# Three units per scan and per product, a smaller fine grid and a transposed residual in a convolution and Mamba kernel

## The reference

```
# layer 0: upsample 64x64 to a fine grid by FFT, pointwise network, low-pass, back to 64x64
h = upsample(x)
h = h @ W1.T + b1                              # 96 -> 384
h = coef[:, 0] + coef[:, 1] * h + coef[:, 2] * (h * h)
h = h @ W2.T + b2                              # 384 -> 96
out = lowpass(h)[::2, ::2]
# layer 1: Mamba over the 4096 positions of a sample
xs, z = split(u @ W_in.T);  xc = silu(causal_conv3(xs) + conv_b)      # 192 channels
dt, B, C = split(xc @ W_x.T);  delta = softplus(dt @ W_dt.T + b_dt)
h_t = exp(delta_t * A) * h_(t-1) + delta_t * B_t * xc_t               # 192 x 16 states
y_t = sum over the 16 states of h_t * C_t
out = ((y + xc * D) * silu(z)) @ W_out.T
```

## Time and profile before

| | |
|---|---|
| time, median of 3 runs (lowest to highest) | 6339.48 us (6336.2 to 6344.21) |
| the profiled execution, first to last instruction | 6343.7 us |
| busy: PE, DVE, POOL, ACT | 6036.5, 5685.5, 5209.8, 5097.3 us |
| DMA moved | 983.25 MB, 155 GB/s |

### The profile page before, as it was taken

How to read it: one execution, slowest core, us unless ns; L and a number is a source line. 1 busy time by engine, 2 the same in 40 slices (tenths; PEclk the granted TensorE clock), 3 DMA queues, 4 the chain that set the end, 5 groups by cost and what they waited for, 6 DMA issues and landing times. The chain is left out here.

```text
span 6343.7 us, 99100 instructions
## 1 busy us (share of the span) xinstructions
PE 6036.5 (95%) x32260; PEld 3123.0 (49%) x32260; DVE 5685.5 (90%) x4459; ACT 5097.3 (80%) x8658; POOL 5209.8 (82%) x5092
## 2 busy tenths in 40 slices
PE   8999999999999999999999999999999999998776
PEld 5645445454554545545455544545455454554222
DVE  0089999999999999999999999999999999999998
ACT  4588888888888888888888788888888888887664
POOL 0078888888888888888888888888888888888988
PEclk9999999999999999999999999999999999998665
DMA  3367676676767667675676767667676766767553
GB/s 95 88 165 170 160 167 157 163 162 169 169 154 168 155 165 170 155 182 142 167 162 162 173 156 169 155 164 163 167 169 156 166 154 165 168 142 160 129 124 75
DMA packets 805826, 983.25 MB, mean 155 GB/s; under 512 B 391258, under 2 KB 417542, under 8 KB 805318
## 3 DMA queue, kind: packets, MB, share of 16 engines
q1 hardware_dynamic: 805318, 976.92, 65.4%
HBM read 717.71 MB, written 259.00 MB: 154 GB/s over the span
## 5 line engine op out<-in xcount | busy, mean ns | idle before, releaser
L1181 POOL TENSOR_TENSOR hc<-hs,cs 128x512 f32<-128x512 f32 x3072 | 3835.6, 1271 | 692.7 <-DVE hs L1140 505.6
L1140 DVE TENSOR_TENSOR_SCAN hs<-av,state,b 128x512 f32<-128x512 f32 x2688 | 3257.8, 1263 | 88.6 <-POOL state L1185 4.9
L1008 ACT ACTIVATE av<-rep_d,nega 128x512 f32<-128x512 f32 x3072 | 2096.7, 713 | 41.5 <-DVE hs L1140 36.8
L1134 DVE TENSOR_TENSOR b<-rep_u,pb 128x1536 f32<-128x1536 f32 x1024 | 1803.5, 1761 | 211.0 <-PE pb L846 124.7
L855 PE MATMUL py<-hc,rsel 128*32 128x512 f32 x6144 | 1141.6, 634 | 40.6 <-POOL hc L1181 39.7
L769 PE MATMUL cb<-xu,w1a 96*128 96x392 f32 x2400 | 984.3, 513 | 27.7 <-DVE b1a L1120 17.4
L774 PEld LDWEIGHTS cb<-w2c,g 128*98 128x98 f32 x9600 | 885.9, 167 | 169.7 <-issue 106.9
L774 PE MATMUL cb<-w2c,g 128*98 128x96 f32 x9600 | 910.7, 252 | 17.4 <-ACT g L956 9.3
L956 ACT ACTIVATE g<-cb,b1a 128x392 f32<-128x392 f32 x1200 | 679.5, 579 | 87.0 <-PE cb L769 78.8
L810 PE MATMUL cb<-xn,wtap 96*96 96x512 f32 x1536 | 723.3, 607 | 2.4 <-ACT xn L1029 2.4
L769 PEld LDWEIGHTS cb<-xu,w1a 96*128 96x128 f32 x2400 | 414.5, 191 | 415.4 <-issue 199.3
(11 more groups left out here) (109 smaller groups left out, 6703.4 us busy)
## 6 DMA issues: line engine op xcount, KB each, us to landing
rep_d<-delta_scratch SPq DMA_DIRECT2D x512, 384.0 KB, 7.0
rep_u<-deltax_scratch SPq DMA_DIRECT2D x512, 384.0 KB, 6.3
cs<-c_scratch SPq DMA_DIRECT2D x512, 256.0 KB, 5.9
delta_scratch<-dlt SPq DMA_DIRECT2D x128, 384.0 KB, 3.1
deltax_scratch<-dlt SPq DMA_DIRECT2D x128, 384.0 KB, 9.2
t1r<-t_scratch SPq DMA_DIRECT2D x160, 240.0 KB, 6.5
v_scratch<-v2s SPq DMA_DIRECT2D x192, 192.0 KB
xb<-in_x SPq DMA_DIRECT2D x128, 192.0 KB, 4.6
```

Of the source, the lines that this page charges most:

```text
L1008: act.activation(av[:, n % NAV, :], rep_d[:, k % 2, j, :], ACT.Exp, scale=nega[:, q, j:j + 1])\
L1134: dve.tensor_tensor(b3[:, :, :], rep_u[:, k % 2, 3 * hf:3 * hf + 3, :], pb[:, None, :].broadcast_to([128, 3, T]), ALU.mult).then_inc(dve_b ...
L1140: dve.tensor_tensor_scan(hs[:, n % NHS, :], av[:, n % NAV, :], b3[:, n % 3, :], start, ALU.mult, ALU.add)\
L1181: pool.tensor_tensor(hc[:, n % NHC, :], hs[:, n % NHS, :], cs[:, k % 2, g % NQ, :], ALU.mult)\
```

## The change

- **Scan and product.** DVE makes one scan of 128x1536 per group, POOL one product of 128x1536. The scan runs through three units, so the state must not leak from one to the next: column 0 of every `av` is set to zero once (ACT fills columns 1 to 511), and column 0 of `b` is written as rep_u * pb + carry by a small scalar_tensor_tensor (128x3) ahead of the product for the other columns. `carry = exp(nega * rep_d[0]) * state` is prepared once per chunk: `first_x` on POOL (at unit 5, it needs the next chunk's rep_d), `first_a` on ACT (unit 15), two products on POOL (units 14 and 23). In a sample's first chunk there is no carry and no small operation. `av` has 9 buffers, so three groups.
- **Grid.** 98 x 97 points: 24 groups of four columns and one of two.
- **Residual.** x1o is transposed into the bank by PE ahead of the two products, in place of a product with the identity behind them; the planner's OUT goes from 2.70 to 2.25.

```
-GW, GH = 100, 98
-NB = GW // 4
+GW, GH = 98, 97
+NB = (GW + 3) // 4
-NHC, NAV, NHS = 6, 8, 6
+NHC, NAV, NHS = 6, 9, 6
...
-    "act": dict(xn=10, y=(18, 6), d=11, mid=23, batch=16),
+    "act": dict(xn=10, y=(18, 6), d=11, mid=23, batch=16, first=15),
-    "pool": dict(u=23, bc=(18, 22), y=(17, 8)),
+    "pool": dict(u=23, bc=(18, 22), y=(17, 8), first=5, carry=(14, 23)),
...  PE, OUT
+                    pe.transpose(o, x1o[:, tb], ident[0:C, 0:C])
                     for t in range(2):
-                        pe.matmul(o, xcs[:, p, t, tb], wo[:, t, :], start=(t == 0), stop=False)
-                    mm = pe.matmul(o, x1o[:, tb], ident[0:C, 0:C], start=False, stop=True)
+                        mm = pe.matmul(o, xcs[:, p, t, tb], wo[:, t, :], start=False, stop=(t == 1), skip_group_check=True)
...
-                act.wait_ge(dve_h, count(dve_h, G * NU + n + 1 - NAV))
-                act.activation(av[:, n % NAV, :], rep_d[:, k % 2, j, :], ACT.Exp, scale=nega[:, q, j:j + 1])\
+                act.wait_ge(dve_h, count(dve_h, G * NG + n // 3 + 1 - NAV // 3))
+                i = (G * NU + n) % NAV
+                act.activation(av[:, i, 1:T], rep_d[:, k % 2, j, 1:T], ACT.Exp, scale=nega[:, q, j:j + 1])\
...
+                lo = 0
+                if k > 0:
+                    lo = 1
+                    dve.wait_ge(pool_carry, count(pool_carry, (s * (NC8 - 1) + k - 1) * 2 + hf + 1))
+                    dve.scalar_tensor_tensor(b3[:, :, 0], rep_u[:, k % 2, js, 0], pb[:, 0:1], carry[:, q, js],
+                                             ALU.mult, ALU.add).then_inc(dve_c, 1)
+                dve.tensor_tensor(b3[:, :, lo:T], rep_u[:, k % 2, js, lo:T],
+                                  pb[:, None, lo:T].broadcast_to([128, 3, T - lo]), ALU.mult).then_inc(dve_bu, 1)
+                dve.wait_ge(pool_st, count(pool_st, G * NG + g + 1 - NHS // 3))
+                dve.wait_ge(act_a, count(act_a, G * NU + n + 3))
...
+                dve.tensor_tensor_scan(hs[:, h:h + 3, :].rearrange("p j t -> p (j t)"),
+                                       av[:, a:a + 3, :].rearrange("p j t -> p (j t)"),
+                                       b3[:, :, :].rearrange("p j t -> p (j t)"), 0.0, ALU.mult, ALU.add)\
...
-                pool.wait_ge(dve_h, count(dve_h, G * NU + n + 1))
-                pool.tensor_tensor(hc[:, n % NHC, :], hs[:, n % NHS, :], cs[:, k % 2, g % NQ, :], ALU.mult)\
+                pool.wait_ge(dve_h, count(dve_h, G * NG + g + 1))
+                pool.tensor_tensor(hc[:, p:p + 3, :], hs[:, h:h + 3, :],
+                                   cs[:, k % 2, q, None, :].broadcast_to([128, 3, T]), ALU.mult).then_inc(pool_hc, 1)
```

More of the change, by code:

```diff
@@ L30, with wide @@
 RING = 3
+def wide(b):
+    return min(4, GW - 4 * b)
 BATCH = 8
@@ L78 @@
 PE_US = {"ST": 0.45, "SA": 0.70, "SB": 0.70, "W_up": 0.70, "W_f": 0.71, "W_2": 2.10, "W_dn": 0.75, "D_lo": 1.20, "D_hi": 1.20,
-         "X": 2.72, "Z": 0.92, "DBC": 1.82, "DT": 0.50, "OUT": 2.70, "WARM": 0.215}
+         "X": 2.72, "Z": 0.92, "DBC": 1.82, "DT": 0.50, "OUT": 2.25, "WARM": 0.215}
 PE_PB, PE_RED = 0.22, 1.00
@@ L295, in build @@
         fcst = hs[:, 4, 0:NF]
-        state = sb("state", [128, NG, 3])
-        zero_state = sb("zero_state", [128, 1])
+        state = sb("state", [128, NQ, NJ])
+        first_x = sb("first_x", [128, NQ, NJ])
+        first_a = sb("first_a", [128, NQ, NJ])
+        carry = sb("carry", [128, NQ, NJ])
         os_ = sb("os_", [128, 4, C])
@@ L500, in _ @@
             load_xb(0, 0)
-            sp.dma_start(up_w[:, :, :], A["up_w"]).then_inc(ld_s, 16)
+            for r in range(2):
+                sp.dma_start(up_w[64 * r:64 * r + 64, :], A["up_w"][64 * r:64 * r + 64, r]).then_inc(ld_s, 16)
             load_xb(0, 1)
@@ L757, in step @@
                 elif name == "W_up":
-                    for e in range(2):
+                    for e in range(wide(b) // 2):
                         i2 = 2 * b + e
@@ L779, in step @@
                         half = slice(HH * (e % 2), HH * (e % 2) + HH)
-                        mm = pe.matmul(bank[half, 0:4 * C], dn_h[:, :], vr[:, e % 2, :], start=True, stop=True)
+                        n = wide(e) * C
+                        mm = pe.matmul(bank[half, 0:n], dn_h[:, :], vr[:, e % 2, 0:n], start=True, stop=True)
                 elif name == "DG":
@@ L824, in batched @@
                 rows = slice(32 + 64 * t, 32 + 64 * t + RANK)
-                return pe.matmul(bank[0:C, :], wdt[rows, C * t:C * t + C], dbc[rows, :], start=True, stop=True)
+                return pe.matmul(bank[0:C, :], wdt[rows, :], dbc[rows, :], start=True, stop=True)
             def out(st, k, bank):
@@ L1038, in c_part @@
             def c_part(st, k, n):
+                if n == AT["act"]["first"] and 0 <= st.s and k + 1 < NC8:
+                    c = st.s * (NC8 - 1) + k
+                    act.wait_ge(pool_first, count(pool_first, c + 1))
+                    act.wait_ge(pool_carry, count(pool_carry, c * 2))
+                    act.activation(first_a[:, :, :], first_x[:, :, :], ACT.Exp).then_inc(act_first, 1)
                 if n == AT["act"]["d"] and 0 <= st.s * NC8 + k + 1 < NS * NC8:
@@ L1138, in unit @@
[L1138 to L1140 removed]
+                    if G == 0:
+                        dve.wait_ge(av_set, count(av_set, 1))
+                dve.wait_ge(pe_b, count(pe_b, G * NG + g + 1))
+                dve.wait_ge(dve_h, count(dve_h, G * NG + g))
+                lo = 0
@@ L1220, in c_part @@
             def c_part(st, k, n):
+                G, ahead_of = st.s * NC8 + k, st.s * (NC8 - 1) + k
+                if n == AT["pool"]["first"] and 0 <= st.s and k + 1 < NC8:
+                    p = (k + 1) % 2
+                    pool.wait_ge(rd_ld[p], count(rd_ld[p], st.s * (4 * 64) + ((k + 1) // 2 + 1) * 64))
+                    pool.wait_ge(act_first, count(act_first, ahead_of))
+                    pool.tensor_tensor(first_x[:, :, :], nega[:, :, :], rep_d[:, p, None, :, 0].broadcast_to([128, NQ, NJ]),
+                                       ALU.mult).then_inc(pool_first, 1)
+                if n in AT["pool"]["carry"] and 0 <= st.s and k + 1 < NC8:
+                    hf = AT["pool"]["carry"].index(n)
+                    js = slice(3 * hf, 3 * hf + 3)
+                    pool.wait_ge(act_first, count(act_first, ahead_of + 1))
+                    pool.wait_ge(pool_st, count(pool_st, G * NG + (hf + 1) * NQ))
+                    pool.tensor_tensor(carry[:, :, js], first_a[:, :, js], state[:, :, js], ALU.mult).then_inc(pool_carry, 1)
                 if n not in AT["pool"]["y"]:
```

87 lines of the change are left out of this document (48 added, 39 removed).

## The result

The changed kernel takes 8441.6 us (median of 4 runs, 8436.4 to 8454.7) against 6337.8 of the kernel before: 1.332 times as long, interval 1.3301 to 1.3338. The profiled execution spans 8452.9 us. I had forecast 6270.

The account below looks back on a forecast made before the run. PE and DVE were taken as nearly level, PE bounding 5 chunks of a sample and DVE 3. 14 x (6.5 - 2.7) + 8 + 5 + 3 = 69 us off 6343.7, less 4.2 for the median: 6270 us, range 6185 to 6455.

Parts of the forecast that it names:

- Column 0: DVE's small scalar_tensor_tensor ahead of b, in 7 of 8 chunks: 0.10 us per group, between 0 and 0.15.
- The second rival: DVE's small operation, with two SBUF tensors, waits wherever POOL is still busy: 2.6 us per chunk, some 6420 us; chance 0.13.
- The wait thus eats its own cause: DVE's scan waits for the third av; PE goes on and repays, so 0.4 of 2.5 us stays, 2.7 per sample.
- the first rival: DVE's wait for the third av stays at 2.5 us, if ACT makes it late: 206 us more, 6476; chance 0.15.
- hidden by 2.8: POOL's first_x at unit 5 waits for rep_d; the state still reaches DVE's scan 2.8 us early.
- Scan and POOL: DVE's one scan of 1536 columns takes 3.41 us; POOL's one product of 1536 takes 3.45, at most 3.8.
- DVE's group: Time from one b to the next on DVE: 5.47 us instead of 5.58, and 5.37 in a first chunk.
- Sum of the gains: Gains on PE and DVE: 6.5 us per middle sample, 8 in the last, 5 in sample 14, some 3 at the start.
- The residual: Transposes for identity products in PE's OUT: 0.45 us saved per chunk, no less than 0, no more than 0.9.
- the grid: 1% fewer columns in PE's W_f and W_2: 0.15 us saved per chunk.
- 3 as DVE's: Three of a sample's eight chunks are bound by DVE, each gaining 0.9 us, with 0.8 more in the first.

## Why the prediction was wrong

The way from the forecast to the result, in runs taken one after the other:

| | us | step |
|---|---|---|
| no carry, waits mended, OUT 2.70 | 6268.5 | |
| OUT at 2.25 | 6346.7 | 78 |
| third av and first_x as in the change | 6482.6 | 136 |
| the operation on column 0 | 8441.6 | 1959 |

- **Column 0: the step that failed.** I wrote "Nearest is the 128x3 product, 0.142; it overlaps with b in part, so between 0 and 0.15, and I take 0.10". Even beside an idle POOL it takes 0.23, and in place it takes 2.74 on average. The row that I took as nearest has one input in PSUM; none of DVE's rows had two tensors in SBUF beside a working POOL, so the row bounded nothing. The second rival named the mechanism and the Trainium skill's rule for it (SBUF — State Buffer, Who interferes with whom), which these runs bear out: two SBUF inputs are held (0.80 and 2.74 us), one is not (0.17 and 0.22). But I priced it "wherever POOL is still busy when a scan ends", 2.6 us per chunk. POOL need not be behind: the scan's end releases its product too. It holds the operation in 744 of the 896 groups, on average over all 2.5 us beyond the idle 0.23, so some 20 us per chunk, not 2.6, and the rival's 6420 should have been over 8000.
- **"The wait thus eats its own cause": wrong.** I kept 0.4 of 2.5 us. With the carry left out the wait stands at 2.1 to 2.6 us in six chunks of eight, nearly the first rival's "whole". ACT was late by its own order; moving the one av took DVE's idle time for av from 179 to 51 us, with the carry in. In the changed kernel itself it is 55 us, near the 40 that I gave, but only because the held operation makes DVE late too: without it, it is 378.
- **first_x, "hidden by 2.8": wrong in one place.** The state copy was in time (6 us of DVE's waits). But I looked only at the products behind first_x on POOL. Once per sample gn stands there too.
- **The planner's OUT: not costed.** I took 2.25 for a number on paper. It moves a W_f ahead of OUT and costs 92 us with the old scans, 78 with the long scan and no carry, and 53 with the carry added in PSUM (6431.6 and 6378.7).
- **Scan and POOL: right, DVE's group only where nothing holds it.** 3.354 and 3.441 us against 3.41 and 3.45. Without column 0 DVE's group is 5.35 us in most of the last sample (b at 6157.89, 6163.24), against 5.37; its mean there is 5.51. So that sample gained 5 us, not the 8 that I had even with column 0's term.
- **Sum of the gains: near by chance.** 6268.5 stands beside my 6270, but that run has no column 0, which my sum had at 0.10 us a group; without it the sum is 6245, by the count given with the run of 6346.7 us. And the terms differ. The residual brought 18 us (I had 32), the grid 33 (13), both 63 (45). The long scan gave 1 us in sample 6, where I had 3.5 from "3 as DVE's", column 0 included.

## What to carry to other kernels

Before an operation is put on DVE beside a working POOL, count its tensors in SBUF: with two of them its price is not its size but what is left of POOL's instruction, and where one semaphore releases both, that can be the whole instruction each time. One tensor in PSUM, or a factor per partition, avoids it. When one instruction replaces three, list what its single wait now gathers, and look through everything queued behind a new waiting instruction, once-per-sample pieces too; and a planner's cost estimate is an edit of the order, to be read in the order itself.

## What the runs showed of the hardware

- One engine can hold up another without a semaphore. I wrote ahead of the prediction that the engines meet only at semaphores; but the small operation has all of its own when its 2.74 us begin, and POOL's product still holds it.
- By its record the small operation on DVE begins 0.047 to 0.057 us before POOL's product in 432 groups (3005.04 and 3005.09 is one) and still ends with it; in 148 groups it begins 0.077 to 0.080 us before (2594.96 and 2595.04) and takes 0.23. The Trainium skill says, of DVE instructions with two SBUF inputs too, that whichever of DVE and POOL starts first gets the shared ports for the whole instruction (SBUF — State Buffer, SBUF: two separate sides). The 148 agree with that; the 432 show that an earlier start in DVE's record alone does not tell who was first.
- A hold shows in DVE's trace as busy time: 2451 us that look like work, with no releaser named, where 896 operations of 0.23 would be some 207.
- A pause of 2.13 us on PE in one group went with a granted clock of 0.71 over the next one, in which PE was busy throughout; after that it was 1.00 again.
